# First half of a layer's normalisation moved in between the expert tiles, weight rounding moved into the attention behind them

## What is computed

```python
x = x + _L0_ffn_ref(_layernorm(x, axis=-1), L0_ffn_w_gate, L0_ffn_w_in, L0_ffn_w_out)
x = x + _L1_attn_ref(_layernorm(x, axis=-1), L1_attn_Wq, L1_attn_bq, L1_attn_Wk, ...)
# in _L1_attn_ref:
q = jax.nn.softmax(to_heads(q), axis=-1)
k = jax.nn.softmax(to_heads(k), axis=-1)
comp_q = 1.0 - q
comp_k = 1.0 - k
...
attn = branch(qf, kf) + branch(comp_qf, comp_kf)
```

## Time and profile before

| | before |
|---|---|
| time, median of 3 runs | 514.51 us (512.66 to 514.63) |
| the profiled execution | 513.1 us |
| its span, first to last instruction | 511.4 us |
| mean granted clock of TensorE | 0.952 |
| busy: TensorE, VectorE, ScalarE, GpSimd | 446.8, 344.9, 308.5, 144.2 us |

### The profile page before, as it was taken

One profiled execution on the slowest core, in us unless ns is written; L12 is line 12 of the kernel. 1 busy time (PEld: TensorE's weight loads), 2 busy tenths in 40 slices (PEclk: granted clock), 3 DMA queues, 4 the chain that ended last, 5 costly groups with the idle time before them and its releaser, 6 DMA issues.

```text
span 511.4 us, 8389 instructions
## 1 busy us (share of the span) xinstructions
PE 446.8 (87%) x2660; PEld 343.3 (67%) x2660; DVE 344.9 (67%) x943; ACT 308.5 (60%) x602; POOL 144.2 (28%) x210
## 2 busy tenths in 40 slices
PE   2898999969883997589898867999999999999994
PEld 1576777648532786447777646778778787878783
DVE  3567777596597654557768845858686777767653
ACT  1676777531443542037565537788777878787881
POOL 7282202122256000125544420222222222222221
PEclk9999999998995998859999978999999999999999
DMA  8224441000400000001111001020202011020201
GB/s 298 63 60 127 140 121 32 0 1 2 164 1 0 1 1 1 0 18 27 33 30 32 13 0 72 13 84 0 83 1 82 10 72 51 32 82 3 84 1 41
DMA packets 14050, 23.98 MB, mean 47 GB/s; under 512 B 4000, under 2 KB 10784, under 8 KB 12608
## 3 DMA queue, kind: packets, MB, share of 16 engines
q1 hardware_dynamic: 13584, 22.71, 13.9%
q10 hardware_dynamic: 432, 0.85, 0.4%
HBM read 19.29 MB, written 0.59 MB: 39 GB/s over the span
## 4 chain that ended last, share of the span: by engine, by line
PE 34%; issue 7%; DVE 5%; ACT 3%; POOL 2%; DMA 2%; SPq 1%; POOLq 0%; DVEq 0%
PE ps L1652 5%; PE ps L1653 4%; PE ps L1654 4%; PE ps L1665 4%; PE ps L1664 4%; PE ps L1663 4%; POOL xnT L500 2%; DMA bigr<-qk 2%; PE ps L1310 2%; DVE masked L900 2%; PE ps L1353 1%; SPq L311 1%; PE ps L1320 1%; PE ps L1620 1%; ACT bigr L762 1%
## 5 line engine op out<-in xcount | busy, mean ns | idle before, releaser
L1156 DVE TENSOR_TENSOR bigr<-ps,bigr 128x512 fp32r<-128x512 f32 x128 | 86.2, 688 | 53.7 <-ACT ps L763 53.7
L762 ACT ACTIVATE bigr<-ps,b 128x512 fp32r<-128x512 f32 x128 | 90.0, 703 | 35.3 <-PE ps L1654 35.3
L624 ACT ACTIVATE big<-ps 128x512 f32<-128x512 f32 (+1 forms) x128 | 68.9, 549 | 46.2 <-PE ps L1320 44.5
L763 ACT ACTIVATE ps<-ps,b 128x512 f32<-128x512 f32 x128 | 86.8, 678 | 0.0
L500 POOL TENSOR_TENSOR xnT<-xnT,big 128x512 f32<-128x512 f32 x32 | 41.4, 1295 | 154.4 <-DVE big L1164 154.4
L1310 PE MATMUL ps<-bigr,qk 128*128 128x256 f32 (+1 forms) x256 | 62.6, 331 | 6.7 <-DVE nmax L907 2.8
L1652 PE MATMUL ps<-k1hi,w1hi 128*128 128x512 f32 x128 | 53.4, 417 | 3.3 <-ACT xnT L519 2.7
L1310 PEld LDWEIGHTS ps<-bigr,qk 128*128 128x128 f32 x256 | 40.3, 195 | 21.2 <-issue 11.1
L907 DVE TENSOR_REDUCE nmax<-ps 128x2 f32<-128x512 f32 x64 | 42.6, 687 | 17.4 <-PE ps L1310 16.9
L1653 PE MATMUL ps<-k1hi,w1lo 128*128 128x512 f32 x128 | 51.3, 401 | 0.0
L1654 PE MATMUL ps<-k1lo,w1hi 128*128 128x512 f32 x128 | 51.3, 401 | 0.0
(11 more groups left out here) (193 smaller groups left out, 801.6 us busy)
## 6 DMA issues: line engine op xcount, KB each, us to landing
big<-gates SPq DMA_DIRECT2D x8, 1024.0 KB, 4.6
bigr<-qk SPq DMA_DIRECT2D x112, 32.0 KB, 1.9
wi<-in_wi SPq DMA_DIRECT2D x4, 512.0 KB, 4.3
wo<-in_wo SPq DMA_DIRECT2D x4, 512.0 KB, 4.4
big<-in_sel SPq DMA_DIRECT2D x1, 1024.0 KB, 8.7
wo<-in_w SPq DMA_DIRECT2D x1, 1024.0 KB, 4.8
wi<-in_w SPq DMA_DIRECT2D x1, 1024.0 KB, 6.9
x<-in_x SPq DMA_DIRECT2D x1, 512.0 KB, 4.4
```

The source lines that it names most:

```text
L624: act.activation(prob[:, h % 8, c], ps[:, 2 + h % 2, c], ACT.Exp, scale=DH ** -0.5).then_inc(s(L + "_exp"), 1)
L762: act.activation(ghi[:, u % 2, c, :], ps[:, c, :], ACT.Gelu_apprx_tanh, bias=b1[:, u % E1, c:c + 1])
L763: act.activation(ps[:, c, :], ps[:, c, :], ACT.Gelu_apprx_tanh, bias=b1[:, u % E1, c:c + 1]).then_inc(s("ff1_gel"), 1)
L1156: v.tensor_tensor(glo[:, u % 2, c, :], ps[:, c, :], ghi[:, u % 2, c, :].bitcast(f32), ALU.subtract).then_inc(s("ff1_glo"), 1)
```

## The change

VectorE: the statistics of `at1`'s first half move from behind tile 4's addition to behind tile 3's, and its normalisation from behind the last tile to behind tile 5's addition. GpSimd: the first half's reciprocal root moves from behind its last tile to behind its addition of tile 4. ScalarE: the first half's evacuation (with the wait for the attention's constants) moves ahead of its share of the last tile; `exponentials(0)` moves ahead of the second half's evacuation; the weights of experts 1, 2 and 3 are rounded one at a time, behind `complements(0)`, `turned_values(2)` and `turned_values(3)`. TensorE: its order stays; `qkv_tiles(0)` waits for the scalings of seven tiles instead of eight, since the banks that it writes were last read by the seventh. No instruction is added or left out, and no transfer changes.

```diff
 # gpsimd, the loop over n
+                if n == NT // 2:
+                    rstds("at1", 0)
-            for hf in range(2):
-                rstds("at1", hf)
+            rstds("at1", 1)
 # scalar, the loop over n
                 last.then_inc(s("ff0_pa"), 1)
-            rounded_weights(range(1, E1))
+                if n == NT - 2:
+                    act.wait_ge(s("ld_at1"), 8 * 16)
+                    evacuate_xnT("at1", 0, QT)
 # scalar, the attention
-            act.wait_ge(s("ld_at1"), 8 * 16)
-            evacuate_xnT("at1", 0, QT)
             turned_values(0)
+            exponentials(0)
             evacuate_xnT("at1", 1, QT + 1)
-            exponentials(0)
             turned_values(1)
             complements(0)
+            rounded_weights(range(1, 2))
             queries(0, 0)
             exponentials(1)
             queries(0, 1)
             complements(1)
             turned_values(2)
+            rounded_weights(range(2, 3))
             queries(1, 0)
             exponentials(2)
             queries(1, 1)
             result(0)
             turned_values(3)
+            rounded_weights(range(3, E1))
 # vector, the loop over n, with m = n - 1
-                    if m == NT // 2:
+                    if m == NT // 2 - 1:
                         ln_stats("at1", 0)
+                    if m == NT // 2 + 1:
+                        ln_normalise("at1", 0)
             ln_stats("at1", 1)
-            ln_normalise("at1", 0)
             ln_normalise("at1", 1)
 # tensor, qkv_tiles(0)
-                    pe.wait_ge(s("ff0_pa"), NT)
-                    pe.wait_ge(s("ff0_pd"), NT)
+                    pe.wait_ge(s("ff0_pa"), NT - 1)
+                    pe.wait_ge(s("ff0_pd"), NT - 1)
```

## The result

| | before | after |
|---|---|---|
| time, median | 514.34 us (510.51 to 515.13) | 516.92 us (515.60 to 521.37) |
| ratio to before, 95% interval | | 1.0071 (1.0045 to 1.0097) |
| the profiled execution | 513.1 us | 515.67 us |
| its span | 511.4 us | 513.9 us |
| mean granted clock of TensorE | 0.952 | 0.946 |

The kernel became slower by 0.7%. A second set of runs of the same changed kernel gave 1.0066 (1.0039 to 1.0093), so the loss is 3.4 to 3.7 us; the medians in the table alone differ by 2.6 us, which both intervals still hold. The time lies in the forecast's range, but the likeliest case, no change within 0.5%, was wrong.

The account below looks back on a forecast made before the run. VectorE bounds the expert tiles and TensorE the attention, with VectorE's wait for TensorE setting the joint's pace. Adding +1.5 us gave 514.6 on the profiled 513.1 and 516.0 on the median; middle 515.3, range 512.9 to 517.5.

Parts of the forecast that it names:

- the likeliest case: Whole kernel: time within 0.5% (2.6 us) of before, chance 0.76; slower by more 0.18, faster by more 0.06.
- VectorE's and GpSimd's part: Layer 0's last expert tiles: addition to x of tile 4 loses 0.65 us beside GpSimd's; first normalisation comes at 155.8.
- Last reduction: VectorE's last expert tile: due at 160.65 instead of 157.29, VectorE ready about 1.85 us sooner but waiting for the chain.
- `project(0)`: First attention step on VectorE: at 167.1 instead of 166.19, with the 2.43 us wait for TensorE gone.
- The rounded weights: Six ScalarE instructions moved into the attention, three pairs of 1.04 us: cost nothing as long as TensorE bounds that stretch.
- The rival with ScalarE's weights laid open: In the attention, all three weight pairs delay TensorE by 3.1 us: +4.6 in total, 518.4 us; chance 0.10.
- The clock at the joint: TensorE's second projections, from 168.55: clock at 0.5 of full, losing 1.7 to 2.7 us.
- the two bounds: How long TensorE's clock stays low from 168.55: 3.7 us or 5.8 us, from two stretches in the earlier trace.
- forecast of +1.5 for the joint: From expert tiles to attention: clock loss 1.7 to 2.7 less 0.7 gain gives +1.0 to +2.0, middle +1.5 us.
- The step that failed: Attention from 172.11: TensorE runs almost without a gap, so a shift of its start shifts the end equally.
- The clock's term: Second projections at the joint: each slow microsecond loses 0.46 at ratio 1.86, together 1.7 to 2.7 us.
- the base: Whole kernel's starting time: 513.8 us, the middle between the profiled 513.1 and the three timed runs' median 514.51.

Follow-up runs that it names:

- tile-first kernel: The changed kernel with ScalarE's evacuation of the first half behind its share of the last tile instead of ahead of it: 1.0001 (0.9978 to 1.0023).
- weights-only kernel: The kernel before with only the rounding of the three experts' weights moved into the attention, as in the change: 1.0016 (0.9994 to 1.0037).
- the delayed one: The kernel before with two useless VectorE additions (0.9 us) ahead of the first turned queries: 1.0022 (1.0000 to 1.0043).
- the timed runs with the third gap filled: One unread product in the 1.47 us TensorE gap of the attention's last batch: changed kernel 1.0015, kernel before 0.9989.

## Why the forecast was right at the joint and wrong in the sum

**VectorE's and GpSimd's part was right.** First normalisation forecast at 155.8, found at 155.79. The addition to x of tile 4 took 1.28 us against 0.58, a loss of 0.70 where 0.65 stood; it ends 0.14 us behind the GpSimd addition that ran from 151.66 for 1.27 us. The Trainium skill, "SBUF — State Buffer", section "Who interferes with whom", has the two engines shut each other out of a shared port pair for such operations; this row agrees. Last reduction forecast at 160.65, found at 160.38, after a wait of 1.62 us (forecast 1.85). ScalarE stood 3.74 us (about 4).

**`project(0)`**: forecast 167.1, found at 166.77, with no wait for TensorE, as said. The tile-first kernel shows the cause that was named: without the evacuation in front of the last tile the reduction's wait goes.

**The rounded weights** cost nothing that shows, as forecast: the pairs start at 173.81, the second batch's heads are normalised 2.0 us later than before, and TensorE does not wait for them at 178.43. The rival with ScalarE's weights laid open, 3.1 us, falls by the weights-only kernel (0.8 us, at most 1.9).

**The clock at the joint** was low at the second projections, as forecast, and came back at 171.2, 3.6 us after their start; that is close to the lower of the two bounds (3.7 and 5.8; read from the earlier trace rows, the second should be 6.0). From the second projections to the first turned queries it took 4.49 us instead of 3.04, 1.45 us lost where 1.7 to 2.7 stood. The first turned queries came at 172.72, 0.61 later than before; the forecast had 1.0 to 2.0.

**The profile of before was late at the joint.** In the weights-only kernel and in the kernel before with a product in the third gap, which have the same joint as before, the first turned queries come 1.23 and 1.03 us sooner than in the profile of before, because the clock came back sooner; in the delayed one, its 0.9 us taken off, 0.93 sooner. Against these the changed joint is 1.5 to 1.8 us later, and the timed runs with the third gap filled say 1.3. The forecast of +1.5 for the joint comes close to these, but in part by luck: it was worked out against one late execution, and against that one it was 0.61, outside the forecast's 1.0 to 2.0. The same profile was lucky in the last stage. The clock from 317 to 321 before, after, and in the weights-only kernel:

```profile
317.00:321.00 4.00, 4.00 (x19) 3.24 (x18) 1.87 (x3) 4.00 (x8) 0.00 (x0) 1.00 0.66 262
```
```profile
317.00:321.00 4.00, 4.00 (x13) 3.14 (x12) 1.38 (x2) 3.27 (x6) 0.00 (x0) 0.63 0.71 242
```
```profile
317.00:321.00 4.00, 4.00 (x16) 3.19 (x15) 2.14 (x4) 2.70 (x5) 0.00 (x0) 0.79 0.28 115
```

All other profiles but one have such a fall in that stage, between 311 and 328, whatever the order at the joint. So the 2.5 us by which the two profiles' spans differ are not the measured loss in small: -0.64 upstream, +0.61 at the joint, +0.37 to the addition to x, +0.46 to the first gelu, and +1.70 from the last stage, which the change does not touch. That they sum to about the right size is chance.

**The step that failed** is the last sentence of the first part: "From 172.11 on TensorE runs almost without a gap through the attention; a shift of that start is a shift of the end." The gap of 0.42 and 1.47 us in the last batch was passed over, and so was the fall behind it, both of which stand in the trace of before (TensorE, and two windows of the clock):

```profile
192.51 0.44 PE L1578 MATMUL ps<-ident,big 128*128 128x128 f32 x2 [0.42 <-DVE big L1084]
194.42 1.13 PE L1537 MATMUL ps<-turn,big 128*128 128x256 f32 x4 [1.47 <-DVE big L1055]
195.39 1.79 PE L1546 MATMUL ps<-big 128*128 128x258 f32 x4
```
```profile
195.50:196.00 0.50, 0.50 (x3) 0.45 (x3) 0.00 (x0) 0.41 (x1) 0.00 (x0) 0.63 0.00 0
199.00:199.50 0.50, 0.50 (x6) 0.50 (x5) 0.00 (x0) 0.00 (x0) 0.00 (x0) 0.95 0.00 0
```

Nothing is late there, and so it has no place in a sum of shifts; but TensorE may leave it at half speed. What it does then costs 2.6 us (the changed kernel against the one with the product there). All five profiles with the changed joint and nothing in that gap have the fall; of the three with the joint of before and no products, one has it (the profile of before). With the kernel before's 0.6 us from the product, some 2 us are left that the change adds behind the joint. That is an estimate, with an uncertainty of about as much. The clocks of the timed runs point the same way: the time at the lower level, (1 - mean clock) x 2 x span, averages 55 us in the changed kernel and 49 with the product; in the kernel before it is 52 in the runs beside it, and 50 with the product. The 1.3 us of the joint and these 2.0 add up to the whole loss because they are differences of the same runs; the sum confirms neither. The clock's term was right in kind and counted at one place where it acts at two.

A smaller part of the miss is the base. The sum started from 513.8, half way between one profile and the median of three runs, and the kernel before measured 514.34: that is 0.5 of the 1.6 us by which 516.92 lies above 515.3.

**What decides the fall at the third gap was not tested.** A slow second projection does not decide it alone: the tile-first kernel and the kernel before with eight products had full clock there and fell all the same. Of 15 profiles with that gap open, 9 have the fall. The Trainium skill, "TensorE: Matmul & The Clock Gate", Part 1, says that the activity monitor runs freely, so that the moment of a change depends on how the work falls against it. That fits a gap of one length which is followed by either clock, and a joint that moves the chances. The profiles bear the moment out as far as they go. From the clock's last return to the end of the gap it is 23.0 to 23.7, 26.1 and 30.5 us in eight profiles with the fall, and 28.0 to 28.8 and 31.6 us in four without; in the other three the last return lies over 70 us back. With the changed joint the clock comes back only at the end of the slow second projections, and from there to the gap TensorE's work follows almost without a wait: 23.0 to 23.4 us in all five profiles, each with the fall. With the joint of before it comes back earlier: 26.1 us in the profile with the fall, 28.0 and 28.7 in the two without. So the change would bind the gap to a bad moment; that is read from the profiles, and no run moved the gap alone. A kernel with the joint of before and many profiles of it would tell its share of falls directly.

## What to carry to other kernels

When an early step is put into another engine's loop, look at what stands behind its wait in that engine's queue: here one evacuation held up the last tile of three engines, and putting it behind the tile gave everything back. Count TensorE's standing times over the whole stage behind an edit, not only where work is late: a gap that costs nothing at full clock may cost more than itself in slow work behind it, and one short product in it is a cheap test, and here a cheap cure. Do not take one profile of each kernel as the difference: set the places against several profiles with the same order.

## What the runs showed of the hardware

- TensorE fell to the lower clock after 0.42 and 1.47 us of standing with 0.44 us of work between them (194.60 in the profile after), half a microsecond into the work that followed, and stayed there for 3.4 us of nearly unbroken work. In the earlier trace rows the gap ahead of the fall was 2.4 us.
- With one product of 0.88 us in that gap the clock stayed full in all four profiles that have it. Only in the changed kernel with nothing at the joint does the gap end where others fell, 23.4 us after the clock's last return; in the other three it ends 27.9, 28.5 and 31.9 us after it, close to the 28.0 to 28.8 and 31.6 us at which profiles without a product kept the clock too.
- A 128x512 product of 4-byte values takes 0.88 us at full clock and leaves two records in the trace.
